# A five-layer graph network: the last two groups' attention features computed between the first chunk's masks, and a chunk's sum, reciprocal and product moved from GpSimd to VectorE

## The reference

```
h = x @ W.T;  alpha_s = h @ a_src;  alpha_d = h @ a_dst
e = leaky_relu(alpha_s[src] + alpha_d[dst], 0.2)
ex = exp(e - segment_max(e, dst)[dst]);  z = segment_sum(ex, dst)
out = segment_sum(h[src] * (ex / z[dst])[:, None], dst) + b
```

## Time and profile before

| | us |
|---|---|
| median of 3 runs | 817.02 (815.36 to 817.50) |
| the profiled execution | 815.22 |
| its span in the profile | 813.4 |
| PE, DVE, ACT, POOL busy | 737.5, 605.7, 463.6, 23.0 |
| preparation 1, from the first weight product to the first mask | 458.4 to 479.3 |
| attention 1, from the first mask to the last product | 479.3 to 592.6 |
| preparation 2, from the norm's end to the first mask | 599.6 to 624.3 |

### The profile page before, as it was taken

One profiled execution on the slowest core, in us unless ns is written; L12 is line 12 of the kernel. 1 busy time (PEld: TensorE's weight loads), 2 busy tenths in 40 slices (PEclk: granted clock), 3 DMA queues, 4 the chain that ended last, 5 costly groups with the idle time before them and its releaser, 6 DMA issues. The chain is left out here.

```text
span 813.4 us, 21039 instructions
## 1 busy us (share of the span) xinstructions
PE 737.5 (91%) x8477; PEld 680.7 (84%) x8477; DVE 605.7 (74%) x1364; ACT 463.6 (57%) x911; POOL 23.0 (3%) x27
## 2 busy tenths in 40 slices
PE   8888888888998999999999849999964999997997
PEld 6656666657997999999999749999963999996997
DVE  7999999997447345533444689999978989996732
ACT  2888898893004023212122668999666899973600
POOL 2000000000000000000000000111000011100000
PEclk9999999999998999999999979999965999999999
DMA  4000000000995000000000410666651099996901
GB/s 143 13 12 12 13 7 1 2 2 16 398 415 205 2 2 1 2 2 2 2 14 26 127 35 21 226 226 212 212 193 52 18 194 195 211 205 188 178 26 36
DMA packets 121661, 78.14 MB, mean 96 GB/s; under 512 B 98088, under 2 KB 116058, under 8 KB 121432
## 3 DMA queue, kind: packets, MB, share of 16 engines
q1 hardware_dynamic: 121216, 75.89, 33.5%
q10 hardware_dynamic: 344, 0.85, 0.3%
HBM read 30.46 MB, written 25.79 MB: 69 GB/s over the span
## 5 line engine op out<-in xcount | busy, mean ns | idle before, releaser
L1896 PE MATMUL banks<-loose,adjacency 128*128 128x194 f16 x1250 | 213.2, 248 | 0.0
L663 PE MATMUL banks<-y_sb,adjacency 128*128 128x192 f16 (+1 forms) x1875 | 165.2, 248 | 1.0 <-DVE h_sb L910 0.8
L663 PEld LDWEIGHTS banks<-y_sb,adjacency 128*128 128x128 f16 x1875 | 160.7, 98 | 1.8 <-DVE h_sb L910 1.0
L486 PEld LDWEIGHTS counts<-hot_code,hot_row 128*128 128x128 f16 x1568 | 93.5, 101 | 61.5 <-DVE hot_code L361 35.9
L1895 PE MATMUL banks<-x_sb,gat_masks 128*128 128x194 f16 x820 | 142.1, 249 | 1.8 <-DVE adjacency L1802 1.8
L486 PE MATMUL counts<-hot_code,hot_row 128*128 128x100 f16 (+3 forms) x1568 | 123.1, 219 | 20.2 <-DVE hot_code L361 14.4
L1866 ACT ACTIVATE gat_masks<-y_sb,node_scalars 128x640 bf16<-128x640 f32 x164 | 121.9, 828 | 4.0 <-PEq L117 4.0
L1896 PEld LDWEIGHTS banks<-loose,adjacency 128*128 128x128 f16 x1250 | 122.7, 98 | 0.4
L361 DVE TENSOR_TENSOR hot_code<-codes_iota,unpacked 128x600 f16<-128x600 f16 x196 | 96.9, 556 | 0.0
L604 ACT ACTIVATE adjacency<-counts 128x800 f16<-128x800 f32 x98 | 81.5, 832 | 17.2 <-PE counts L486 17.1
L1895 PEld LDWEIGHTS banks<-x_sb,gat_masks 128*128 128x128 f16 x820 | 80.6, 98 | 3.6 <-DVE y_sb L1798 1.9
(11 more groups left out here) (238 smaller groups left out, 1020.5 us busy)
## 6 DMA issues: line engine op xcount, KB each, us to landing
kept_adj<-adjacency SPq DMA_DIRECT2D x5, 4000.0 KB, 31.8
adjacency<-kept_adj SPq DMA_DIRECT2D x25, 800.0 KB, 9.2
y_sb<-a_dst_rows SPq DMA_DIRECT2D x10, 320.0 KB, 3.7
window_keys<-edge_keys SPq DMA_DIRECT2D x187, 5.0 KB
residual<-h_sb SPq DMA_DIRECT2D x5, 240.0 KB, 2.0
kept_x<-x_sb SPq DMA_DIRECT2D x1, 1200.0 KB, 4.6
loose<-residual SPq DMA_DIRECT2D x5, 240.0 KB, 3.5
x_sb<-kept_x SPq DMA_DIRECT2D x5, 240.0 KB, 4.9
```

Of the source, the lines that this page charges most:

```text
L486: last = nc.tensor.matmul(counts[:, 2 * (p % HELD) + i, start:end], hot_row[:, q % 2, b * QUAD + w, :], hot_codes(q % 2, b)[:, w, start - ...
L663: return nc.tensor.matmul(k.ps[:, j % G, 0:cols], k.ADJ[:, i, j * P:(j + 1) * P], y[:, i, 0:cols], start=i == 0, stop=i == NT - 1)
L1896: return nc.tensor.matmul(bank[:, 2 * BC:4 * BC], under_of(x)[:, q * P:(q + 1) * P], features[1][:, i, :], start=False, stop=i == NT - 1)
```

## The change

Seven edits belong together:

1. `high`, `low` and `scaled` become functions that `attend` can call. Of the last two groups (3 and 4), the rounding and the low half of group 3, and all of group 4's tables, are made in `attend`: ACT calls high(3) behind the mask of tile 3 and high(4) behind the mask of tile 12; DVE calls low(3) behind unit 4, scaled(4) behind unit 5 and low(4) behind unit 7. In the preparation, low(2) and scaled(3) move behind the extremes.
2. One of the two f32 scratch tables lies in `H`, so the mask slot there is held back until step 22, and ACT waits at step 22 for the last low half. PE waits for the low halves at tiles 0, 5, 10, 15 and 20 of the first chunk.
3. `largest` of the last group reads the product in PSUM; ACT copies that product out only behind it.
4. The row of alpha_d is turned, copied and stored in two parts. The first two groups' part goes early, and the loads for the first two chunks need that part only. SP stores the second part behind those loads, and waits for it.
5. The turned input has memory of its own.
6. Of 22 `keep_busy` matmuls at the start of `attend`, 12 move to the preparation's end, 6 stay and 4 go.
7. The join, reciprocal and product of the first three chunks go from POOL to DVE, in the units with tiles 12, 17 and 21.

```diff
@@ prepare_attention: DVE
+        source = tiles(k.Hg, g) if g < NG - 1 else products(g)
+        if g < NG - 1:
+            dve.wait_ge(s.emptied_a, g + 1)
...
         for g in range(NG):
             evict(g)
-            if g >= 2:
-                low(g - 2)
+            if 2 <= g < NG - 1:
+                low(dve, g - 2)
+            if 1 <= g < NG - 1:
+                scaled(dve, g - 1)
             if g >= 1:
-                scaled(g - 1)
                 largest(dve, g - 1)
...
         dve.tensor_scalar(ext[:, 3:4], ext[:, 3:4], SMALL / LARGEST, None, ALU.mult).then_inc(s.extremes, 1)
-        low(NG - 2)
-        scaled(NG - 1)
+        low(dve, NG - 3)
...
         dve.tensor_scalar(ext[0:4, 5:9], k.ident[0:4, 0:4], ext[0:4, 4:5], None, ALU.mult).then_inc(s.ex_diag, 1)
-        low(NG - 1)
+        scaled(dve, NG - 2)
@@ prepare_attention: ACT
+        def copy_rows(part):
+            act.wait_ge(s.ad_turned, part + 1)
+            rows = destinations[part]
+            nc.scalar.activation(rows[:, :], k.ps[0:rows.shape[0], (6, 2)[part], 0:P], ACT.Copy).then_inc(s.ad_copied, 1)
...
             if g >= 2:
-                high(g - 2)
+                high(act, g - 2)
+            if g == NG - 1:
+                copy_rows(0)
+        act.wait_ge(s.sized, NG)
+        empty(NG - 1)
         factor(NG - 1)
-        empty(NG - 1)
-        act.wait_ge(s.ad_turned, 1)
-        nc.scalar.activation(HT[0][0:NT, 0:P], k.ps[0:NT, 2, 0:P], ACT.Copy).then_inc(s.ad_copied, 1)
+        copy_rows(1)
         nc.scalar.activation(k.in_norm[:, :], k.a_d[:, :], ACT.Exp, scale=1 - SLOPE).then_inc(s.exp_ready, 1)
-        high(NG - 2)
-        high(NG - 1)
@@ prepare_attention: SP
         sp.wait_ge(s.ad_copied, 1)
-        sp.dma_start(d.a_dst, HT[0][0:NT, 0:P]).then_inc(s.ad_stored, 16)
+        sp.dma_start(d.a_dst[0:2 * G, :], destinations[0][:, :]).then_inc(s.ad_stored, 16)
         sp.wait_ge(s.ad_stored, 16)
         for ch in range(2):
             load_destinations(k, d, sp, ch, k.row_ready[ch])
+        sp.wait_ge(s.ad_copied, 2)
+        sp.dma_start(d.a_dst[2 * G:NT, :], destinations[1][:, :]).then_inc(s.ad_stored, 16)
+        sp.wait_ge(s.ad_stored, 32)
@@ prepare_attention: PE
+            if g == 3:
+                pe.wait_ge(s.emptied_d, 2)
+                nc.tensor.transpose(k.ps[0:2 * G, 6, 0:P], k.a_d[:, 0:2 * G], k.ident[:, :]).then_inc(s.ad_turned, 1)
...
+        keep_busy(nc, k, 0, 12)
@@ attend
+JOINED, INVERTED = 6, 10
+HIGH_AFTER, LOW_AFTER, SCALED_AFTER, SCALED_UNTIL = (3, 12), (4, 7), 5, 22
...
-            given, held_to = [], [0] * len(slots)
+            given, held_to = [], [0] * (len(slots) - 1) + [SCALED_UNTIL]
@@ attend: DVE, in the loop over the units
-                if ch == NG - 1 and first <= DRAINED[G - 1] + 1 < first + n:
-                    write(ch - 1)
-                if 0 < ch < NG - 1 and first <= DRAINED[G - 1] + SUMMED_AFTER < first + n:
-                    invert(ch - 1)
+                for part, at in ((join, DRAINED[G - 1] + 1), (invert, DRAINED[G - 1] + JOINED), (write, DRAINED[G - 1] + INVERTED)):
+                    if ch and first <= (at if ch < NG - 1 else DRAINED[G - 1] + 1) < first + n:
+                        part(ch - 1)
+                if u == LOW_AFTER[0]:
+                    k.low_of(dve, NG - 2)
+                if u == SCALED_AFTER:
+                    k.scale_of(dve, NG - 1)
+                if u == LOW_AFTER[1]:
+                    k.low_of(dve, NG - 1)
@@ attend: ACT
+            if x == SCALED_UNTIL:
+                act.wait_ge(k.low_ready, 2 * NG)
...
+                if x in HIGH_AFTER:
+                    k.high_of(act, NG - 2 + HIGH_AFTER.index(x))
@@ attend: PE
+                if ch == 0 and i % G == 0:
+                    pe.wait_ge(k.low_ready, 2 * (i // G + 1))
...
-            keep_busy(nc, k, 1, 22)
+            keep_busy(nc, k, 1, 6)
@@ attend: POOL
-            with pool.Else():
-                small_gpsimd(pool)
```

More of the change, by code:

```diff
@@ L1233, in largest, with scaled, low, high @@
     def largest(dve, g):
[L1235 to L1237 removed]
+        source = tiles(k.Hg, g) if g < NG - 1 else products(g)
+        if g < NG - 1:
+            dve.wait_ge(s.emptied_a, g + 1)
+        dve.tensor_reduce(size[:, g:g + 1], source[:, :, 0:C], axis=mybir.AxisListType.XY, op=ALU.max,
+                          apply_absolute_value=True).then_inc(s.sized, 1)
+    def scaled(dve, g):
+        dve.wait_ge(s.emptied_a, g + 1)
+        dve.wait_ge(s.exp_ready, 2 * (g + 1))
+        if g == 0 and first:
+            dve.wait_ge(k.residual_stored, NG * 16)
+        if g == 0 and first:
+            dve.wait_ge(s.turned, 2)
+        for a in range(2):
+            if g:
+                dve.wait_ge(s.low_ready, 2 * (g - 1) + a + 1)
+            dve.tensor_tensor(scratch[a], tiles(k.Hg, g)[:, :, 0:BC], group(factors[a], g).unsqueeze(2).to_broadcast([P, G, BC]),
+                              ALU.mult).then_inc(s.t_ready, 1)
+    def low(dve, g):
+        for a in range(2):
+            dve.wait_ge(s.high_ready, 2 * g + a + 1)
+            into = tiles(features[a], g)
+            nc.vector.scalar_tensor_tensor(out=into[:, :, BC:2 * BC], in0=scratch[a], scalar=FEATURE_SCALE, in1=into[:, :, 0:BC],
+                                           op0=ALU.mult, op1=ALU.subtract).then_inc(s.low_ready, 1)
+    def high(act, g):
+        if g == 0 and first:
+            act.wait_ge(k.x_stored, 16)
+        for a in range(2):
+            act.wait_ge(s.t_ready, 2 * g + a + 1)
+            nc.scalar.activation(tiles(features[a], g)[:, :, 0:BC], scratch[a], ACT.Copy, scale=FEATURE_SCALE).then_inc(s.high_ready, 1)
     def turned_banks(g):
@@ L1272, in evict @@
             dve.tensor_copy(group(k.a_s, g), products(g)[:, :, C]).then_inc(s.emptied_d, 1)
[L1274 to L1292, removed]
         chain(dve.memset(k.Hg[:, :, C:C + 1], 1.0))
@@ L1340, in _ @@
         chain(dve.tensor_scalar(k.wide[0:1, 0:1], ext[0:1, 0:1], ext[0:1, 9:10], SMALL, ALU.max, ALU.is_gt))
+    k.low_of, k.scale_of, k.high_of, k.low_ready = low, scaled, high, s.low_ready
+    k.late = s.emptied_a, s.exp_ready, s.t_ready, s.high_ready, s.low_ready
     @block.scalar
@@ L1844, in small_vector @@
                 add(NG - 1, q)
-            write(NG - 1)
+            for part in (join, invert, write):
+                part(NG - 1)
             for n in range(MEASURED_EARLY + 1, NC + 1):
@@ L2281, in _ @@
                 nc.clear_and_free_semaphores(built)
-        passed = [s for s in k.held if s not in k.row_ready]
+        passed = [s for s in k.held if s not in (*k.row_ready, *k.late)]
         k.adj_first, *k.adj_back = semaphores(nc, k, "reload", "first " + " ".join(f"back_{m}" for m in range(NG)))
```

32 lines of the change are left out of this document (11 added, 21 removed).

## The result

The changed kernel takes **822.31 us** (median of 7 executions, 819.51 to 824.61), the kernel before 815.85 beside it (7 executions, 814.66 to 817.50). The ratio is 1.0078, with a 95% interval of 1.0063 to 1.0093: 6.5 us slower (5.1 to 7.6). The prediction was 823.4, slower.

What follows compares the result with a forecast made beforehand. The prediction took PE to bound attention, with DVE and ACT nearly full; for each attention -3.1 + 5.9 + 0.8 - 0.4 = +3.2, twice +6.4, giving 823.4 us. The range was 817 to 829, the forecast's own 820 to 827.

Steps and rivals of the forecast that it cites:

- The tail: Preparation's end: DVE loses six instructions, so the barrier comes 3.1 us earlier for each attention, bounds 2.6 and 3.4.
- DVE is last: At the barrier ending the preparation: the upper bound, 3.4 us gained, if DVE finishes last.
- The first chunk: Attention's first chunk: inserted work and the held slot delay masks and tiles 10 and 16; 5.9 us lost, bounds 3.5 and 6.5.
- The slot wait: First chunk, tile 10's mask: ACT waits about 0.6 us for tile 0's slot, as the one in `H` is held back.
- (a): Rival on the first chunk: the masks have room, inserted work hides under PE, only the tail's gain is left; 810, chance 0.12.
- (b): Rival on the first chunk: low(3) and the slot cost nothing, loss 3.5 cancels the gain; 817, chance 0.12.
- The clock: PE in the first chunk: waits may drop the granted clock to half rate, costing 0.8 us for each attention, bounds 0 and 2.5.
- the second hole: First chunk, PE without work from 16.5 to 20.2 us behind the first mask; a clock fall there would cost 1.4.
- The joins: Chunks 2 and 3: join and product on DVE instead of POOL gain 0.4 us for each attention, bounds -0.5 and 0.8.
- The stall of PE behind it shrinks by some 0.2, in chunks 2 and 3: PE's wait behind the join: shorter by some 0.2 us in each of the two chunks, giving the 0.4 gained.
- Moving the loads earlier by itself gives nothing: Preparation: earlier destination loads gain 0, since the rows are read only at the first mask, which waited for the barrier.

Runs made afterwards that it cites:

- holes filled: Changed kernel with spare matmuls added at two places of the first chunk where PE waits, 16 before tile 3's first blocks and 30 before tile 10: 819.89 us.
- experiment 3: Changed kernel with ACT's high(4) behind the mask of tile 15 instead of tile 12: 816.21 us, ratio 1.0000.
- experiment 7: Changed kernel with high(3) behind the mask of tile 9, high(4) behind that of tile 15 and scaled(4) one unit earlier: 812.00 us, ratio 0.9944.
- experiment 4: Changed kernel without high, low and scaled of the last two groups in attention, their tables constant; only attention 1 readable: first chunk 28.66 us.
- experiment 5: Kernel before with only the last mask slot in `H` held back until step 22: 816.27 us, ratio 0.9993.
- experiment 8: Changed kernel with both stores of the row ahead of the destination loads: 825.60 us, ratio 1.0121.

## Why the prediction was right

It said 823.4, where 822.3 was measured, and for the stated reason. The 1.1 between them is nearly all in the time of the kernel before, which was 817.02 in three executions and 815.85 in seven; the difference that was forecast is 6.4, and 6.5 was measured. So close a hit is luck, as two terms were off in opposite senses. Point by point, for one attention with its preparation:

- **The tail, -3.1: measured -3.36 and -3.25.** DVE's six instructions are right (`wide` 3.45 earlier). PE and the store ended 0.3 sooner than they had been placed: in the times of the kernel before (0.65 less than the changed one's), PE's spare matmuls ended at 475.48 and not 475.8, and the store landed at about 475.4 and not 475.7. With DVE's end at 475.32 that is near the upper bound, "DVE is last". (The pair of scaled was counted as 1.3 in placing L1333; its pitch makes it 1.14, and the place came out right all the same.)
- **The first chunk, +5.9: measured +6.30 and +5.93, and +5.92 with the holes filled.** The table of times held all along. From the first mask, scaled(4) was due to give its first table at T = 14.5, and high(4) started at 14.83; over(7) was due at 17.9 and came at 18.2; tile 10 at 20.15 and came at 20.57; the end at 33.3 and came at 33.71. Two parts were off, in opposite senses. The slot wait is 0.61 to 0.70 at full rate, but 1.39 and 1.02 in the two attentions of the profiled execution, not 0.6; and ACT stood at high(4) for 2.87 and not 3.4. The second part of the loss follows from the first: what ACT loses at the slot it no longer waits at high(4). Experiments 3 and 7 show that the loss is in the order of the insertions more than in their amount. ACT's long stand at high(4) is 2.2 of it, the places of high(3) and scaled(4) are some 1.8, and in the better order the same work costs 2.1. Rivals (a), 810, and (b), 817, fail for this order. The time of (b) is what experiment 3 measures with another one, and experiment 7, 812, lies between the two.
- **The clock, +0.8, bounds 0 and 2.5: measured 1.2** (2.4 us between the kernel with its holes filled and the changed one), 1.6 by the two ratios. The place was right, the second hole. Its price there was worked out as 1.4, and five falls cost 1.6 on average. The 0.8 that was taken has no working of its own; that the fall came in five holes of eight, at 1.6 each, makes it 1.0. The Trainium skill's rule, TensorE: Matmul & The Clock Gate (HAM oscillation — how this bites in real kernels), gave a sum 1.2 higher, 824.6; the runs bear it out in most of the holes and not in all. What the prediction did not have is the start: with 6 spare matmuls instead of 22 PE stays at half rate until 488.6 (0.72 over 488 to 489), 12.0 us behind the first mask, where it had been 4.9. It was costed at nothing. By experiments 4 and 5 it costs about 0.8 in attention 1 without the inserted work (1.25 less the 0.47 of the slot), and with the work in it about 0.4 (33.71 against 33.33). Giving the matmuls back won that 0.4 in attention 2 and nothing in attention 1, where PE fell in the next hole, and the long hole took it back in both.
- **The joins, -0.4, bounds 0.5 and -0.8: measured -1.1, outside.** This is the step that failed in size. "The stall of PE behind it shrinks by some 0.2, in chunks 2 and 3": it did not shrink, it went, and chunks 2 and 3 became 0.35 shorter each. The bracket's 0.19 had been taken as its price, but the two matmuls around it start 0.44 apart (538.12 and 538.56) at a pitch of 0.083, so it cost 0.36. A third wait went with them, worth 0.33, in front of the turning of finished tiles in the last chunk, on which the prediction had not looked.
- **The sum.** -3.3 + 5.9 + 1.2 to 1.6 - 1.1 gives 2.7 to 3.1 for one attention, 5.4 to 6.2 in all; measured 6.5, with an interval of 5.1 to 7.6. The clock's and the joins' errors, +0.4 to +0.8 and -0.7, cancelled.

"Moving the loads earlier by itself gives nothing" was not run alone. The sentence left out the other half, which experiment 8 shows: the shorter tail needs the early loads.

## What to carry to other kernels

Work that is moved from a serial stretch into a pipelined one costs by its place in each engine's order more than by its amount: here the same ten instructions (four roundings on ACT, six on DVE) cost each attention 5.9 us or more in one order and 2.1 in another. An instruction that is to wait for another engine goes behind as much independent work as its engine still has, so look, for each inserted wait, at when its input can be there at the earliest, and at what stands behind it. Where a change has one part that gains and one that loses, as here the joins and the order, run them apart: the kernel with the joins alone (813.7) and the one with the other order (812.0) both beat the one that it replaced.

## What the runs showed of the hardware

The granted clock is not a fixed answer to a hole. Eight holes of 2.8 to 3.55 us in PE's work lowered it to 0.50 in five cases, and the chunks with a fall were 1.1 to 2.4 us longer. Shorter ones did it too: 2.00 us in the run with 22 spare matmuls, 2.51 in the changed kernel, while 1.84 did not. The executions of the kernel with such holes spread by 5.1 us (819.5 to 824.6), and by 1.6 once they are filled, but the kernel without them also spread by up to 5.0. Half rate can also last long when PE works with gaps: 13.7 us in the changed kernel (474.9 to 488.6), with PE busy 7.14 of 10 us in the middle of it. An elementwise sum of 128 x 485 in f32 took 1.88 us on POOL, part of which may be a wait for DVE (the over of 534.28 was still running when it began; that wasn't tested), and 0.66 on DVE. While POOL was at it a DVE instruction lasted 1.56 us instead of 1.15, and 1.94 beside POOL's product.
